# Top-2 expert routing moved into the attention stage: per-expert regions, one list of 72 tiles, results scattered by token, and the sum and norm in the stage after

## The reference, cut to what matters

```python
p = softmax(x @ gate_w.T)                 # 8 experts
for e in the 2 largest of p:
    y += p[e] * (relu(x @ w1[e] + b1[e]) @ w2[e] + b2[e])   # hidden width 512
x2 = layernorm(x + y)
```

## Time and profile before

| | us |
|---|---|
| median of 3 runs | 1625.65 (1625.34 to 1627.88) |
| the profiled execution, its own time | 1632.78 |
| its span, first to last instruction | 1631.1 |
| first attention | 0 to 419.3 |
| routing of the first mixture | 419.3 to 515.7 |
| its experts | 515.7 to 684.2 |
| its combination | 684.2 to 739.0 |
| projection of the delta stage | 739.0 to 929.8 |
| the rest | 929.8 to 1631.1 |

### The profile page before, as it was taken

One profiled execution on the slowest core, in us unless ns is written; L12 is line 12 of the kernel. 1 busy time (PEld: TensorE's weight loads), 2 busy tenths in 40 slices (PEclk: granted clock), 3 DMA queues, 4 the chain that ended last, 5 costly groups with the idle time before them and its releaser, 6 DMA issues. The chain is left out here.

```text
span 1631.1 us, 35495 instructions
## 1 busy us (share of the span) xinstructions
PE 1048.3 (64%) x13683; PEld 825.7 (51%) x13684; DVE 855.5 (52%) x2199; ACT 611.6 (37%) x1135; POOL 229.2 (14%) x284
## 2 busy tenths in 40 slices
PE   5888888996502999703666495883676676503960
PEld 2666666664502999701333275882454454503960
DVE  3566666764141444393777494112777676131436
ACT  1355555455101555403777322111543443102530
POOL 0000000000036506160111101100000000043015
PEclk9789889888555999956777696665766755556985
DMA  2000000000721324132221304114111210701213
GB/s 72 2 15 21 9 15 22 21 15 8 282 77 65 101 71 111 52 85 65 52 52 45 103 3 60 22 19 112 33 46 39 71 44 8 260 32 53 64 48 93
DMA packets 165845, 96.55 MB, mean 59 GB/s; under 512 B 61937, under 2 KB 155217, under 8 KB 164817
## 3 DMA queue, kind: packets, MB, share of 16 engines
q1 hardware_dynamic: 158928, 79.95, 16.9%
q0 software_dynamic: 6784, 14.69, 2.9%
HBM read 55.81 MB, written 38.80 MB: 58 GB/s over the span
## 5 line engine op out<-in xcount | busy, mean ns | idle before, releaser
L1015 ACT ACTIVATE be_h<-be_up,be_cur 128x128 f32<-128x128 f32 x320 | 91.3, 368 | 143.1 <-PE be_up L994 143.1
L480 ACT ACTIVATE a_at<-a_scores 128x1280 f32<-128x1280 f32 x64 | 78.9, 1233 | 58.1 <-PE a_scores L365 58.0
L976 PE MATMUL be_down<-b_w,be_h 128*128 x640 | 88.9, 282 | 1.4 <-ACT be_h L1015 0.4
L994 PE MATMUL be_up<-be_xT,be_cur 128*128 128x128 f32 x640 | 86.9, 279 | 0.4 <-DVE be_xT L1035 0.3
L360 PE MATMUL a_scores<-a_rk,a_kx 32*128 32x128 f32 x1024 | 70.9, 349 | 25.3 <-ACT a_at L480 19.2
L1029 DVE TENSOR_SCALAR be_cur<-b_w 128x516 f32 x80 | 35.3, 441 | 91.8 <-issue 89.4
L976 PEld LDWEIGHTS be_down<-b_w,be_h 128*128 128x128 f32 x640 | 77.7, 191 | 5.4 <-issue 3.9
L994 PEld LDWEIGHTS be_up<-be_xT,be_cur 128*128 128x128 f32 x640 | 78.9, 194 | 2.4 <-issue 1.9
L360 PEld LDWEIGHTS a_scores<-a_rk,a_kx 32*128 32x128 f32 x1024 | 49.0, 217 | 59.5 <-issue 32.8
L611 DVE TENSOR_TENSOR a_at<-a_at,a_con 128x256 f32<-128x256 f32 x128 | 48.6, 421 | 49.6 <-ACT a_at L480 47.9
L409 POOL DMA_DIRECT2D rows<-a_xo x8 | 6.2, 781 | 407.7 <-DVE a_xo L601 407.7
(11 more groups left out here) (360 smaller groups left out, 2678.5 us busy)
## 6 DMA issues: line engine op xcount, KB each, us to landing
sorted_b<-br_zero SPq DMA_DIRECT2D x8, 640.0 KB, 8.5
be_xs<-sorted_b SPq DMA_DIRECT2D x20, 256.0 KB
results_b<-be_ys SPq DMA_DIRECT2D x20, 256.0 KB, 2.3
b_w<-in_b_w SPq DMA_DIRECT2D x16, 256.0 KB, 9.5
g_X<-rows SPq DMA_DIRECT2D x16, 256.0 KB, 5.0
d_w<-in_d_w SPq DMA_DIRECT2D x16, 256.0 KB, 5.9
sorted_d<-dr_zero SPq DMA_DIRECT2D x4, 640.0 KB, 6.9
de_xs<-sorted_d SPq DMA_DIRECT2D x10, 256.0 KB
```

Of the source, the lines that this page charges most:

```text
L480: op(at[m % 2][:].rearrange("p g q k -> p g (q k)"), S4[:, :, 0:320], ACT.Copy).then_inc(s_ata, 1)
L976: i = mm(BY[u % 2][:, 0:P], h[u % 2][:, f, :], w2[:, bass.ds(e, 1), f, :].rearrange("p e c -> p (e c)"), start=(f == 0), stop=(f == FC - 1))
L994: i = mm(BU[u % 2][:, f * P:(f + 1) * P], cur[u % 2][:, f * P:(f + 1) * P], xT[u % 2][:], start=True, stop=True)
L1015: i = op(h[u % 2][:, f, :], BU[u % 2][:, f * P:(f + 1) * P], act_fn, bias=cur[u % 2][:, FC * P + f:FC * P + f + 1])
```

## The change

- The gate's logits, the two largest, the counts and the places of a token are computed in `lion_stage`, two steps after its group: PE adds eight small products per step and a count of two products, ACT two small instructions, DVE `choose` (slot 0), `counted` and `dispatch` (slot 4). The gate's logits come from the products before the norm, and are corrected with the mean and the deviation.
- POOL copies the normalized rows once and scatters them with eight indirect DMAs per group into one region per expert (4224 rows of 130 words: the row, the number of the token and its weight). SP stores the rows in POOL's place. In the last steps SP loads the experts' weights, and at the end it writes eight blocks of padding.
- One list of 72 tiles takes the place of 80: full tiles of each expert, and a dummy tile for what is left over.
- `expert_stage` loads each tile by itself on SP, with its number from a register. DVE's `result` has three instructions for one: the bias, a cast of the token's number, the weight. POOL scatters each tile by token.
- `moe_route` and `moe_combine` are gone for the first mixture. `delta_project` loads three parts for one, POOL adds them (`row_sum`) and normalizes (`row_norm`), DVE and ACT make the statistics; SP stores the normalized rows.
- The constants are loaded in part: for the first attention 806 KB, for others from 64 KB on.
- The attention's loop is written out for three steps ahead of it, and delta_project's for three steps behind it; before, each had one step ahead and one behind.

```diff
+REGION = TOK + P
+DUMMY = NE * REGION // P
+ROW = P + 2
+SKIP = 4 * TOK
+NT_TOP2 = 2 * TOK // P + NE
...
+            for n in range(3):
+                step(n, n % 2, (n + 1) // 2, n == 0, False)
+            with eng.Fori(1, NG // 2 - 1) as it:
...
+                if not isinstance(n, int) or n > 1:
+                    sp.wait_ge(s_out, 16 * (n - 1))
+                sp.wait_ge(s_xo, n)
+                sp.dma_start(one(o_rows, n - 1), xo[1 - b][0][:, :, 0:P]).then_inc(s_out, 16)
...
+            for dst, src in route["weights"]:
+                sp.dma_start(dst, src).then_inc(s_mw, 16)
+            step(NG - 1, 1, rows_in=False, residual_in=False)
+            step(NG, 0, rows_in=False, residual_in=False)
+            sp.wait_ge(s_tab, 1)
+            for e in range(NE):
+                end = sp.value_load(ends[0:1, e:e + 1], min_val=0, max_val=e * REGION + TOK)
+                sp.dma_start(route["regions"][bass.ds(end, P), :], pad[:]).then_inc(s_pads, 16)
+            sp.wait_ge(s_out, 16 * NG)
+            sp.wait_ge(s_mw, 16 * len(route["weights"]))
+            sp.wait_ge(s_pads, 16 * (1 + NE))
...
+            def yn_logits(out):
+                for t in range(GT):
+                    i = mm(out(t), yn[:, t * P:(t + 1) * P], wog[:], start=True, stop=True, skip_group_check=True)
+                return i
+            def x_logits(out):
+                for t in range(GT):
+                    o = 1 + (t % 2) * P
+                    i = mm(out(t), xp[:, t // 2, o:o + P], gw[:], start=True, stop=True, skip_group_check=True)
+                return i
...
+                return mm(out, C["ones"], c2[:].rearrange("p t e -> p (t e)"), start=False, stop=True, skip_group_check=True)
+            spare = lambda t: S4[:, t, 320:320 + NE]
...
+                    if m == 2 and not first:
+                        yn_logits(spare)
+                    if m == 3 and not last:
+                        x_logits(spare)
+                    if m == 4 and (not isinstance(n, int) or n >= 2):
+                        pe.wait_ge(s_pick, n - 1)
+                        count(S4[:, 0, 320:320 + NE * (GT + 1)])
...
+            def scatter(n, b):
                 pool.wait_ge(s_xo, n + 1)
-                nc.gpsimd.dma_start(one(o_rows, n), xo[b][:]).then_inc(s_out, 16)
...
+                nc.gpsimd.tensor_copy(xo[b][1][:, :, 0:P], xo[b][0][:, :, 0:P]).then_inc(s_xb, 1)
+                pool.wait_ge(s_slot, n + 1)
+                pool.wait_ge(s_xb, n + 1)
+                for k in range(2):
+                    for t in range(GT):
+                        nc.gpsimd.indirect_dma_start(route["regions"], bass.IndirectOffsetOnAxis(ap=seat[b][:, k, t:t + 1], axis=0),
+                                                     xo[b][k][:, t, :], None).then_inc(s_scat[b], 16)
+            for n in range(NG):
+                scatter(n, n % 2)
+            for b in range(2):
+                pool.wait_ge(s_scat[b], 64 * NG)
...
+                    wide = 320
+                    if (m == 2 and not first) or (m == 3 and not last):
+                        wide += NE
+                    if m == 4 and (not isinstance(n, int) or n >= 2):
+                        op(places[:], S4[:, 0, 320:320 + NE * (GT + 1)], ACT.Copy)
+                    op(at[m % 2][:, :, 0:wide], S4[:, :, 0:wide], ACT.Copy).then_inc(s_ata, 1)
+                    if m == 1 and (not isinstance(n, int) or n >= 2):
+                        top_exps(n - 2)
...
+            experts = C["experts"].unsqueeze(1).unsqueeze(1).broadcast_to([P, 2, GT, NE])
+            def choose(n, b):
+                of_tile = lambda a: a.unsqueeze(2).broadcast_to([P, GT, NE])
+                then(v.tensor_tensor(lg[:], of_tile(mv[:, :, 0]), gsum[:].unsqueeze(1).broadcast_to([P, GT, NE]), ALU.mult))
+                then(v.tensor_tensor(lg[:], rl[:], lg[:], ALU.subtract))
+                then(v.tensor_tensor(lg[:], lg[:], of_tile(rsv[:]), ALU.mult))
+                for t in range(GT):
+                    i = own.mark(v.max(top[:, t, :], lg[:, t, :]))
+                dve.wait_ge(s_dve, i)
+                for t in range(GT):
+                    i = own.mark(v.max_index(idx[:, t, :], top[:, t, :], lg[:, t, :]))
+                dve.wait_ge(s_dve, i)
+                then(v.tensor_copy(se[:], top[:, :, 0]))
+                v.tensor_tensor(top[:], top[:], of_tile(se[:]), ALU.subtract).then_inc(s_top, 1)
+                then(v.tensor_copy(idf[:].rearrange("p k t -> p t k"), idx[:, :, 0:2]))
+                then(v.tensor_tensor(pick[:], experts, idf[:].unsqueeze(3).broadcast_to([P, 2, GT, NE]), ALU.is_equal))
+                then(v.tensor_tensor(c0[:, 2:], pick[:, 0], pick[:, 1], ALU.add))
+                then(v.tensor_tensor(c1[:, 2:], c0[:, 2:], c0[:, 1:1 + GT], ALU.add))
+                v.tensor_tensor(c2[:, 1:], c1[:, 2:], c1[:, 0:GT], ALU.add).then_inc(s_pick, 1)
+            def counted(before, totals):
+                then(v.tensor_tensor(pl[:], before.rearrange("p (t e) -> p t e", t=GT),
+                                     run[:].unsqueeze(1).broadcast_to([P, GT, NE]), ALU.add))
+                return v.tensor_tensor(run[:], run[:], totals, ALU.add)
+            def dispatch(n, b):
+                then(v.tensor_tensor(mine[:], pick[:], pl[:].unsqueeze(1).broadcast_to([P, 2, GT, NE]), ALU.mult))
+                then(v.tensor_reduce(pf[:], mine[:], AX_X, ALU.add))
+                dve.wait_ge(s_tex, n + 1)
+                then(v.tensor_reduce(se[:], tex[:], AX_X, ALU.add))
+                then(v.reciprocal(se[:], se[:]))
+                for k in range(2):
+                    v.tensor_tensor(xo[b][k][:, :, P + 1], tex[:, :, k], se[:], ALU.mult)
+                    v.tensor_copy(xo[b][k][:, :, P], tok[:, GT * k:GT * k + GT])
+                v.tensor_copy(seat[b][:], pf[:]).then_inc(s_slot, 1)
+                dve.wait_ge(s_slot, n + 1)
+                then(v.tensor_scalar(tok[:], tok[:], float(GTOK), None, ALU.add))
...
+                if not isinstance(n, int) or n >= 2:
+                    dve.wait_ge(s_out, 16 * (n - 1))
+                    dve.wait_ge(s_scat[b], 32 * GT * earlier)
...
+                    if m == 2 and not first:
+                        then(v.tensor_tensor(rl[:], at[0][:, :, 320:320 + NE], xg[1 - b][:], ALU.add))
+                    if m == 3 and not last:
+                        v.tensor_copy(xg[1 - b][:], at[1][:, :, 320:320 + NE])
+                    if m == 4 and (not isinstance(n, int) or n >= 2):
+                        then(counted(places[:, 0:NE * GT], places[:, NE * GT:]))
                     for q in (2 * h, 2 * h + 1):
...
                         i = v.tensor_tensor(d, d, C["diag"].unsqueeze(1).broadcast_to([P, 4, 64]), ALU.mult)
                     i.then_inc(s_atd, 1)
+                    if m == 0 and (not isinstance(n, int) or n >= 2):
+                        choose(n - 2, b)
+                    if m == 4 and (not isinstance(n, int) or n >= 2):
+                        dispatch(n - 2, b)
...
+            own.restart(dve)
+            choose(NG - 2, 0)
             sums(NG - 1, 1, NG // 2 - 1)
-            norm(NG - 1, 1)
+            dve.wait_ge(s_rl, 1)
+            v.tensor_tensor(rl[:], X0[:, 0:NE * GT].rearrange("p (t e) -> p t e", t=GT), xg[1][:], ALU.add)
+            dve.wait_ge(s_cnt, 1)
+            then(counted(X1[:, 0:NE * GT], X1[:, NE * GT:NE * (GT + 1)]))
+            dispatch(NG - 2, 0)
+            norm(NG - 1, 1, NG // 2 - 1)
+            choose(NG - 1, 1)
+            dve.wait_ge(s_cnt, 2)
+            then(counted(X1[:, P:P + NE * GT], X1[:, P + NE * GT:P + NE * (GT + 1)]))
+            then(v.tensor_tensor(cnt[:], run[0:1, :], C["region"][0:1, :], ALU.subtract))
...
+            dispatch(NG - 1, 1)
...
+            then(v.tensor_tensor(le[:], base[1][:, 4:].unsqueeze(1).broadcast_to([1, NT_TOP2, NE]),
+                                 j_of.unsqueeze(2).broadcast_to([1, NT_TOP2, NE]), ALU.is_le))
+            v.tensor_reduce(ef[:, 0], le[:], AX_X, ALU.add)
...
+            then(v.tensor_scalar(ef[:, 1], ef[:, 1], float(DUMMY), None, ALU.min))
+            v.tensor_copy(route["expert"][:], ef[:, 0])
+            v.tensor_copy(route["tile"][:], ef[:, 1]).then_inc(s_tab, 1)
...
+        @block.sync
+        def _(sp):
+            def load(j, u):
+                at = sp.value_load(tile[0:1, bass.ds(j, 1)], min_val=0, max_val=DUMMY)
+                sp.dma_start(xs[u][:], row_tiles[bass.ds(at, 1)].rearrange("t p c -> (t p) c")).then_inc(s_in[u], 16)
+            sp.dma_start(ident[:], consts[:, columns]).then_inc(s_c, 16)
+            for u in range(U):
+                load(u, u)
+            def body(g, last):
+                for u in range(U):
+                    if not last:
+                        sp.wait_ge(s_y, g * U + u + 1)
+                        load(g * U + U + u, u)
+            rounds(sp, body)
...
+        @block.gpsimd
+        def _(pool):
+            def body(g, last):
```

(87 more changed lines are left out.)

382 lines of the change are left out of this document (295 added, 87 removed).

## The result

The changed kernel takes 1576.22 us (median of four runs, 1570.52 to 1584.49) where the kernel before took 1626.77 beside it: a ratio of 0.9685, with a 95% interval of 0.9634 to 0.9737. It is faster, by 51 us and not by the 83 forecast, and lies outside the range of 1516 to 1570. The profiled execution took 1576.39 us with a span of 1574.5.

What follows compares the result with a forecast made beforehand. PE was taken to bound the experts, no engine the attention throughout, where PE and DVE meet without slack. Terms −39.1 − 60.3 + 6.3 + 15.8 − 5.8 = −83.1 took 1632.8 to 1549.7, less 7.1 gave 1543 us; range 1516 to 1570.

Steps and rivals of the forecast that it cites:

- the attention's steps and prologue: Attention: added routing work makes the steps 34 us longer (bounds 24 and 46) and the prologue 1.7.
- the attention's end: Behind the attention's last step: last choices, places and eight scatters make the next stage start 21.5 us later.
- the experts with the combination: Experts' start to delta_project's first instruction: 163.0 us instead of 223.3, so −60.3, at 2.12 us a tile.
- the last step of the sum: Whole kernel: 1549.7 lowered to 1542.6, as the profiled execution lay 7.1 us above the median of runs.
- the stages with shorter constants: delta_invert −3.3 us, gate_stage and last mixture −2.5 for both, from shorter loads of constants: sum −5.8.
- I add 0.5 for each of the five for PE at its lower clock after the new gap: Attention steps 2 to 6: 0.5 us each, from four transposes taking 1.09 us at 1.2 GHz against 0.66.
- my 5.3 for work and waits: Full attention step: 3.3 us for `choose`, 1.0 for slots 2 and 3, 1.0 for slot 4.
- the boundary of 2.3 behind the landing of 2.2: Ends of attention and experts: after the last scatter, 2.2 us to land and 2.3 to the next stage.
- 0.3 for a 128x128 norm: delta_project: POOL's normalization of a 128x128 block was taken to last 0.3 us.
- my 0.6: delta_project steps: DVE's convolution loses 0.6 us per us of POOL's work, 13.7 us in all (bounds 0 and 22.8).
- rival 3: delta_project: POOL and DVE exclude each other entirely, +9 us, 1552; 7.2 more with sums at 1.8 us; chance 0.12.
- Rival 2: delta_project: POOL and DVE don't collide, two-input instructions go on untouched, −13.7 us, 1529; chance 0.13.

Runs made afterwards that it cites:

- before_again: The kernel before, unchanged, run once more for a second profile: 1626.60 us.
- choose_later: Changed kernel with the choice of experts behind the three instructions of the mixed input instead of ahead of them: 1567.83 us, ratio 0.9627.
- one_input_sums: Changed kernel with GpSimd's two sums in delta_project replaced by copies, the sum left out: 1568.61 us, ratio 0.9647.
- fill_three: Changed kernel with unread products of 128x512 in all three of PE's waits of an attention step: 1555.69 us, ratio 0.9564.
- choose_split: Changed kernel with the choice in slot 1 behind the sum, statistics in slot 7, PE's second layer waiting for the sum alone: 1537.30 us, ratio 0.9440.

## Why the prediction was right and wrong

**Direction and mechanism held.** The routing and combination stages are gone, PE bounds the experts at 2.14 us a tile (71 results in 151.8 us; forecast 2.12), DVE and POOL stay under it, and the clock there was 0.94, with 0.50 until 502.1 and 1.00 from there to 655.7. Of the 33.6 us between 1542.6 and 1576.2, the attention's steps and prologue make 10.6, the attention's end 4.6, the experts with the combination 10.3, the recurrence 7.5 and the last step of the sum 7.1; delta_project gives back 5.4 and the stages with shorter constants 1.2.

**The step that failed: "I add 0.5 for each of the five for PE at its lower clock after the new gap".** I had priced four transposes at either level and taken them for the whole of what the new gap does. Behind the gap the clock fell for 13.7 us and more, and everything in that stretch ran slower: at a mean clock of 0.79 PE ran at half its rate for two fifths of the step. Steps 2 to 6 cost 45.7 us more and not 29.0; the one with a clock of 0.90 cost 5.0, which is near my 5.3 for work and waits, and filling the wait took the rest away. The other steps and the prologue cost 0.6 and not 6.7, which hides a third of this, and that is luck: the profile of before that I used has a long prologue (first square at 92.3 us, at 85.1 in before_again, at 89.7 in the changed kernel). A second, smaller error in the same part: four small products of logits take 1.06 us at full clock (in choose_later) and 1.88 at the low one, not the 0.66 of transposes. `choose` was sized rightly, 3.2 us for 3.3.

**The end of the attention and of the experts: the boundary of 2.3 behind the landing of 2.2 was mis-sized.** I read the boundary from stages whose last transfer is a plain store. Behind GpSimd's indirect transfers its queue drains for 5.3 and 5.9 us. Spreading the drains gave back 3.5 us at the attention's end, of the 4.6 missing there, and 5.2 at the experts' end, which is all of the 4.8 missing there. The drain of 2.7 us behind the routing's 32 scatters stood in the trace of before, inside the 4.4 us from POOL's last work to 515.66; it was there to read, and I took the 2.3 of the boundary without such transfers. Most of the other half of the experts' miss is the first tile: its result comes 7.1 us after PE's start, at 1.2 GHz, where I had counted one tile's pace and 0.5. PE's start itself came 3.7 us into the stage, where I had estimated 4.5.

```profile
L1522 DVE TENSOR_SCALAR bx_ys<-bx_yb,bx_xs x72: 285/286/290, 502.6 to 654.4; 128x128 f32<-128x128 f32 x72
```

**delta_project: several terms off, partly against each other.** The prologue grew by 8.8 us, not 6.3, and the steps by 7.9, not 15.8, in the profiled execution, where the stage took its shorter length. Where it takes the longer one it grows by 27 us in all, so that my 22.1 lies between the two lengths that I didn't know of. "0.3 for a 128x128 norm": it takes 1.32 us, 5.3 for a group, but costs the convolution nothing. The sums take 1.34 and 1.60, inside the bounds, and cost 2.0 of their 2.9 us, a factor of 0.7 between my 0.6 and the 1 of rival 3. Rival 2, no collision, is right for the norm alone: copies with one input cost 0.35 us each in one_input_sums. Two steps without sums pay nothing.

The Trainium skill (SBUF — State Buffer, Who interferes with whom) states that a VectorE instruction with two SBUF inputs contends with a GpSimd instruction that reads SBUF, and that the order of issue decides who blocks. The traces agree that there is contention in all three cases, but not that the loser waits for the whole of the other instruction: beside a sum of 1.26 us alone VectorE's goes from 0.75 to 1.75 us, beside a copy of 0.61 to 1.09, and beside the norm it keeps its 0.75 us while GpSimd's goes from 0.78 to 1.32, so there the loss is GpSimd's. The order of issue wasn't varied.

**Not seen at all: the recurrence**, 7.5 us in the profiled execution, by code that the change doesn't touch; its cause stays open.

**The last step of the sum, from 1549.7 to 1542.6.** I carried the distance of one profiled execution from the median over to the changed kernel. Its own profiled execution lay at the median (1576.39 and 1576.22). Those 7 us were never the change's. Nor can a measurement here tell 3 us from nothing, as I had it: the four runs of the changed kernel lie 14 us apart, and the interval of the ratio is 0.5% to either side.

## What to carry to other kernels

Before work is put ahead of an instruction that PE waits for, look at PE's granted clock on either side of that wait: here a wait of 2.6 us cost about twice its length again, because the clock was low for 13.7 us and more behind it, and in fill_three and choose_later waits of 2.0 and 1.9 us brought it down from full. Move the work behind what PE needs next, then look for the next thing PE waits for, down to the semaphore: one that covers more than the reader needs (`s_z` for the statistics, where the sum was enough) passes the stall on. Filling the wait with idle products is the weaker cure (49.3 us a step against 46.5), and three fills weren't better than one. Count GpSimd's indirect transfers since its last drain before a barrier, and keep its sums, and where it can be had its copies, from under VectorE's instructions with two inputs.

## What the hardware showed that was not expected

- The drain of GpSimd's queue takes 0.083 us for each indirect transfer since the last drain: 2.66 us for 32, 5.30 for 64, 5.93 for 72, 1.35 for 16, 0.70 for 8.
- Steps with identical instructions took 50.8, 54.8, 55.9 or 58.9 us in one execution, as the clock fell in them, and in the same order in three profiles of four.
- At a granted clock of 1.00 throughout, the step took as long as at 0.93 (49.2 us): beyond what VectorE's chain allows, the clock gained nothing.
- A GpSimd copy with one input slows VectorE's two-input instruction too, 0.75 to 1.09 us; a GpSimd norm beside it is slowed itself instead.
- PE's stops without a visible cause fall at one place of each group of 128 records, and products added in another stage move that place; the same 3840 records took 115.5 to 117.1 us with the stops at 40 to 80 and 118.4 to 125.3 elsewhere.
- One chip ran the kernel before in 1733 us and the relatives of choose_split in 1578 to 1583. In one attention step PE waited 4.0 us ahead of the scores for nothing that the profile shows, where on another chip it waited 1.8.
